# Attention scores on two row groups, exponentials by pairs of batches, and a new order on TensorE

## The reference

```python
q, k, v = per-head maps of plin(xm, w_q, b_q), plin(xm, w_k, b_k), plin(xm, w_v, b_v)
scores = jnp.einsum('bhqd,bhkd->bhqk', qt, kt) / math.sqrt(HD)
attn = jax.nn.softmax(scores, axis=-1)
out_h = expmap0(jnp.einsum('bhqk,bhkd->bhqd', attn, vt))
attn_out = plin(_from_heads(out_h), w_o, b_o)
```

## Time and profile before

| | us |
|---|---|
| median of 3 runs | 1287.87 (1287.47 to 1288.47) |
| profiled execution, its own time | 1287.52 |
| its span, first to last instruction | 1285.7 |
| TensorE busy | 1096.9 (85%) |
| VectorE busy | 1040.2 (81%) |
| ScalarE busy | 853.4 (66%) |
| GpSimd busy | 605.3 (47%) |

### The profile page before, as it was taken

The page is one execution under the profiler, slowest core; times in us unless marked ns, Lnnn a source line. Parts: engine busy times, 40 slices in busy tenths (PEclk is TensorE's granted clock), DMA queues, the critical chain, the costliest instruction groups (busy, mean ns, idle before and its releaser), DMA issues.

```text
span 1285.7 us, 20138 instructions
## 1 busy us (share of the span) xinstructions
PE 1096.9 (85%) x5760; PEld 783.9 (61%) x5782; DVE 1040.2 (81%) x2502; ACT 853.4 (66%) x2310; POOL 605.3 (47%) x1059
## 2 busy tenths in 40 slices
PE   8999967875895499999999999999988688888885
PEld 7888833332442287777777777777776345555554
DVE  6887758887787467888888888888987789989984
ACT  3545467877884246666666666666666788888873
POOL 2345236663575524334433444433421356667764
PEclk9999979997997799999999999999998889989998
DMA  7334221424976333334333433334225346666633
GB/s 246 105 112 103 97 81 45 176 111 144 375 232 187 98 99 82 99 99 98 86 88 91 99 88 89 87 99 99 60 61 127 67 97 164 164 164 165 164 99 115
DMA packets 116287, 156.32 MB, mean 122 GB/s; under 512 B 9296, under 2 KB 99536, under 8 KB 114640
## 3 DMA queue, kind: packets, MB, share of 16 engines
q1 hardware_dynamic: 115632, 155.03, 43.8%
q10 hardware_dynamic: 544, 0.00, 0.0%
HBM read 111.22 MB, written 27.00 MB: 108 GB/s over the span
## 4 chain that ended last, share of the span: by engine, by line
issue 24%; POOL 16%; PE 12%; DVE 9%; ACT 7%; POOLq 0%; DVEq 0%; ACTq 0%
POOL t_qk L1972 5%; POOL t_u L1902 4%; PE t_bk L1395 3%; POOL t_u L1907 3%; PE t_fB L1416 2%; PE t_bk L2034 1%; PE t_fA L2048 1%; ACT t_vbd L1460 1%; DVE t_qt L1628 1%; ACT t_vbd L1476 1%; ACT t_junk L1434 1%; PE t_bk L2022 1%; DVE t_bmax L1635 1%; PE t_fA L1378 1%; ACT t_y L1523 1%
## 5 line engine op out<-in xcount | busy, mean ns | idle before, releaser
L2034 PEld LDWEIGHTS t_bk<-t_vbd,t_pt 128*128 128x128 f32 x1024 | 133.4, 194 | 30.5 <-issue 19.3
L2034 PE MATMUL t_bk<-t_vbd,t_pt 128*128 128x66 f32 x1024 | 131.4, 273 | 18.5 <-ACT t_pt L2152 13.9
L2022 PE MATMUL t_bk<-t_qbd,t_kpar 128*128 128x256 f32 x512 | 135.9, 388 | 0.5 <-DMA t_qbd<-t_qt 0.5
L1395 PE MATMUL t_bk<-k_w12g,t_ut 128*128 128x512 f32 x256 | 126.5, 618 | 2.4 <-ACT t_ut L1516 1.2
L2022 PEld LDWEIGHTS t_bk<-t_qbd,t_kpar 128*128 128x128 f32 x512 | 92.8, 192 | 10.7 <-DMA t_qbd<-t_qt 0.9
L411 POOL TENSOR_SCALAR s_hleak<-s_hring,k_leak 128x128 f32<-128x128 f32 x128 | 47.6, 372 | 100.6 <-ACT s_hring L366 93.6
L2146 ACT ACTIVATE t_ysq<-t_y 128x768 f32<-128x768 f32 x64 | 53.8, 841 | 60.0 <-DVE t_y L2325 60.0
L2048 PE MATMUL t_fA<-k_wqkv,t_ut 128*128 128x512 f32 (+1 forms) x256 | 91.2, 500 | 1.2 <-ACT t_ut L2129 1.2
L1913 POOL TENSOR_SCALAR t_s_su<-t_s_ru 128x4 f32<-128x4 f32 x16 | 3.8, 236 | 180.8 <-ACT t_s_ru L2137 180.8
L2048 PE MATMUL t_fB<-k_wqkv,t_ut 128*128 128x512 f32 (+1 forms) x256 | 88.6, 489 | 0.0
L2152 ACT ACTIVATE t_pt<-t_bk 128x512 f32<-128x512 f32 x128 | 73.7, 587 | 21.7 <-PE t_bk L2022 20.2
(11 more groups left out here) (377 smaller groups left out, 3069.6 us busy)
## 6 DMA issues: line engine op xcount, KB each, us to landing
t_scb<-g_rows SPq DMA_DIRECT2D x64, 256.0 KB, 4.6
t_shb<-g_rows SPq DMA_DIRECT2D x64, 256.0 KB, 5.5
hidden_rows<-k_own SPq DMA_DIRECT2D x6, 1536.0 KB, 5.8
s_xrow<-in_x_dram SPq DMA_DIRECT2D x16, 512.0 KB, 3.6
k_hs<-s_hring SPq DMA_DIRECT2D x16, 512.0 KB, 3.1
b_xin<-in_x_dram SPq DMA_DIRECT2D x16, 512.0 KB, 4.4
x_rows<-b_xout SPq DMA_DIRECT2D x16, 512.0 KB, 5.1
t_xf<-x_rows SPq DMA_DIRECT2D x16, 512.0 KB, 4.7
```

The costliest lines, as they stand in the source:

```text
L1395: last = nc.tensor.matmul(z.fW[:, j, :], z.ut[:, c, j * P:(j + 1) * P], k["w12g"][:, c, :], start=False, stop=(c == C - 1))
L2022: last = nc.tensor.matmul(bk[e % 2][:, c * 4 * T:(c + 1) * 4 * T], kpar[:, c, e, :, :].rearrange("p a t -> p (a t)"), qbd[:, c, :, e * T:( ...
L2034: last = nc.tensor.matmul(bk[2 + e % 2][:, p * VW:(p + 2) * VW], pt[:, e % 2, p * T:(p + 2) * T], vbd[:, j, h, p:p + 2, :].rearrange("p c ...
```

## The change

A pair `n` of batches takes the place of a batch in `scores` and in the exponentials.

- Scores: for each batch and half `c`, instead of one product over 128 rows and 256 columns there are two, over rows 0 to 63 and 64 to 127, with 128 columns each. Rows 0 to 63 go with the pairs of heads 0 and 1 into bank 0, rows 64 to 127 with the pairs 2 and 3 into bank 1 (in the other columns `qbd` is zero in these rows). So both banks are filled by one pair of batches.
- Exponentials: one of 1024 columns over banks 0 and 1 for a pair. There are two tiles for them: `ptile`, of 1024 columns, and the tile `qt`, used again while it holds no queries. The next scores wait for the exponential before.
- Values: the same products, that read the new places.
- Order on TensorE: scores and values by pairs among the four products; the second stage's `turn_u` stands before the last two values in turn 16; the transposes of `qk` come after those of `u` and `o`, all four banks together, row tile by row tile for banks 0 and 1, each waiting for its own part of `qk`.
- Order on ScalarE: the four exponentials stand where those of batches 0, 2, 3 and 5 stood; `ut` is copied before `ot`.
- The numbers in the waits follow the new counts.

```diff
-                def scores(e):
-                    if e == 0:
+                def scores(n):
+                    if n == 0:
                         pe.wait_ge(s["qbd_loaded"], i * (4 * 16))
                         pe.wait_ge(s["kpar_ready"], i * (2 * C))
-                    if e >= 2:
-                        pe.wait_ge(s["exp_ready"], (i - 1) * GB + (e - 1))
-                    for c in range(C):
-                        last = nc.tensor.matmul(bk[e % 2][:, c * 4 * T:(c + 1) * 4 * T], kpar[:, c, e, :, :].rearrange("p a t -> p (a t)"),
-                                                qbd[:, c, :, e * T:(e + 1) * T], start=True, stop=True)
+                    else:
+                        pe.wait_ge(s["exp_ready"], (i - 1) * EPAIRS + n)
+                    for e in (2 * n, 2 * n + 1):
+                        for c in range(C):
+                            for r in range(2):
+                                rows, at = slice(r * T, (r + 1) * T), (e % 2 * C + c) * 2 * T
+                                last = nc.tensor.matmul(bk[r][:, at:at + 2 * T], kpar[rows, c, e, :, :].rearrange("p a t -> p (a t)"),
+                                                        qbd[rows, c, 2 * r:2 * r + 2, e * T:(e + 1) * T], start=True, stop=True)
                     last.then_inc(s["score_ready"], 1)
...
-                for e in range(GB + 1):
-                    if i == NG and e == 7:
-                        once(second.turn_u, 0)
-                    if mid and e < GB:
-                        scores(e)
-                    if mid and e >= 1:
-                        values(e - 1)
-                    if front and e < GT - 1:
-                        products(e + 1)
...
+                if mid:
+                    for n in range(2, EPAIRS):
+                        scores(n)
+                        values(2 * n - 2)
+                        values(2 * n - 1)
+                if i == NG:
+                    once(second.turn_u, 0)
+                if mid:
+                    values(GB - 2)
+                    values(GB - 1)
                 if head:
                     turn_x(i + 1)
...
                 if front:
-                    for b in range(C, 2 * C):
-                        turn_qk(b)
+                    if mid:
+                        pe.wait_ge(s["exp_ready"], i * EPAIRS)
+                    for half in range(2):
+                        for j in range(GT):
+                            if half == 0:
+                                pe.wait_ge(s["qk_ready"], i * GT + j + 1)
+                            for b in (2 * half, 2 * half + 1):
+                                last = nc.tensor.transpose(bk[b][:, j * P:(j + 1) * P], qk[:, j, b * P:(b + 1) * P], k["ident"][:, :])
+                                if j == GT - 1:
+                                    last.then_inc(s["qkt_ready"], 1)
...
-                def exponentials(e):
-                    act.wait_ge(s["score_ready"], (i - 1) * GB + (e + 1))
-                    if e >= 2:
-                        act.wait_ge(s["pv_ready"], (i - 1) * GB + (e - 1))
-                    nc.scalar.activation(pt[:, e % 2, :], bk[e % 2][:, :], ACT.Exp, scale=1.0 / math.sqrt(HD)).then_inc(s["exp_ready"], 1)
+                def exponentials(n):
+                    act.wait_ge(s["score_ready"], (i - 1) * EPAIRS + (n + 1))
+                    if n >= 2:
+                        act.wait_ge(s["pv_ready"], (i - 1) * GB + 2 * (n - 1))
+                    nc.scalar.activation(pt[n % 2], bank[:, 0:2, :].rearrange("p r n -> p (r n)"), ACT.Exp, scale=1.0 / math.sqrt(HD)).then_inc(s["exp_ready"], 1)
```

More of the change, by code:

```diff
@@ L49 @@
 NBLK = D // BLK
+EPAIRS = GB // 2
 QMAX = 127.0
@@ L1530, in turned_xd @@
         elif self.t:
-            act.wait_ge(self.t["score_ready"], NG * GB)
+            act.wait_ge(self.t["score_ready"], NG * EPAIRS)
         for c in range(C):
@@ L1703, in attention_mlp @@
         vbd = m.sb("vbd", [P, GT, 2, PAIRS, VW])
-        pt = m.sb("pt", [P, 2, 2 * D])
+        ptile = m.sb("pt", [P, 4 * D])
         rden = m.sb("rden", [P, 2, PAIRS // 2, 2])
@@ L1751, in attention_mlp @@
         flat_qt = qt[:, :, :].rearrange("p c r -> p (c r)")
+        pt = (ptile[:, :], flat_qt)
         flat_qbd = qbd[:, :, :, :].rearrange("p c q r -> p (c q r)")
@@ L2031, in values @@
                         pe.wait_ge(s["o_ready"], 2 * ((i - 1) * GB + e - 1))
-                    pe.wait_ge(s["exp_ready"], (i - 1) * GB + (e + 1))
+                    pe.wait_ge(s["exp_ready"], (i - 1) * EPAIRS + (e // 2 + 1))
                     for p in range(0, PAIRS, 2):
-                        last = nc.tensor.matmul(bk[2 + e % 2][:, p * VW:(p + 2) * VW], pt[:, e % 2, p * T:(p + 2) * T],
+                        at = (p % 4 // 2 * 4 + e % 2 * C + p // 4) * 2 * T
+                        last = nc.tensor.matmul(bk[2 + e % 2][:, p * VW:(p + 2) * VW], pt[e // 2 % 2][:, at:at + 2 * T],
                                                 vbd[:, j, h, p:p + 2, :].rearrange("p c w -> p (c w)"), start=True, stop=True)
@@ L2050, in products @@
                     last.then_inc(s["qkv_ready"], 1)
[L2052 to L2056, removed]
                 if front:
                     products(0)
-                for e in range(GB + 1):
-                    if i == NG and e == 7:
-                        once(second.turn_u, 0)
-                    if mid and e < GB:
-                        scores(e)
-                    if mid and e >= 1:
-                        values(e - 1)
-                    if front and e < GT - 1:
-                        products(e + 1)
-                if front:
-                    pe.wait_ge(s["qk_ready"], (i + 1) * GT)
-                    if mid:
-                        pe.wait_ge(s["exp_ready"], i * GB)
-                    for b in range(C):
-                        turn_qk(b)
+                if mid:
+                    scores(0)
+                if front:
+                    products(1)
+                if mid:
+                    values(0)
+                    values(1)
+                if front:
+                    products(2)
+                if mid:
+                    scores(1)
+                if front:
+                    products(3)
+                if mid:
+                    for n in range(2, EPAIRS):
[4 more added lines that the diff above has]
+                    once(second.turn_u, 0)
+                if mid:
+                    values(GB - 2)
+                    values(GB - 1)
                 if head:
@@ L2191, in turn @@
                 for e in range(GB):
-                    if mid:
-                        exponentials(e)
+                    if mid and e in (0, 2, 3, 5):
+                        exponentials((0, 2, 3, 5).index(e))
                     if front and e < GT:
@@ L2219, in turn @@
                         scaled_a()
+                if head:
+                    turned_u(i + 1)
+                if i == NG:
+                    once(second.turned_u, 0)
                 if mid:
@@ L2224, in turn @@
                                              fB[:, cc * GR:(cc + 1) * GR].rearrange("p (e c t) -> p e c t", c=C, t=T), ACT.Copy).then_inc(s["ot_ready"], 1)
-                if head:
-                    turned_u(i + 1)
-                if i == NG:
-                    once(second.turned_u, 0)
                 if front:
```

10 lines of the change are left out of this document (5 added, 5 removed).

## The result

| | median of runs | ratio to before, 95% interval |
|---|---|---|
| before | 1288.45 us (9 runs) | |
| after | 1297.42 us (9 runs) | 1.0069 [1.0042, 1.0097] |

A forecast was written before the change was run, and what follows sets the result against it. It took a ring through VectorE, TensorE, ScalarE and GpSimd, 34.02 us a turn, as the bound. First turn -2.0, middle turns -1.0, clock +2.3, last turn -3.0 gave -3.7 on a span of 1285.7: 1284 us, range 1277 to 1308.

The forecast's parts named there:

- Scores: TensorE's score products: a pair of batches falls from 1.72 to 0.87 us, plus about 0.1 for each of two row changes.
- Rival 2: Score products: row groups don't overlap, a pair costs 1.74 + 0.2 us, adding 1.5 a turn; 1307 us, chance 0.26.
- Exponentials: ScalarE: four of 1024 columns at 1.1 us replace eight of 512 at 0.587; 4.4 instead of 4.7 us, beside the ring.
- the ring: Attention turn from T, the first `t_y`: eighth output at 24.39, `kpar` 2.19 later, next `t_y` after 7.44; 34.02 to become 33.95.
- TensorE's tail: Transposes ending a middle turn: eighth output at T+24.13, `kpar` 2.38 later, 0.07 us gained a turn, -1.0 over 14 turns.
- First turn: Turn 0: `qk` is turned part by part, `kpar` starts at about 452.4 instead of 454.81; -2.0 us.
- The clock: TensorE's gap before the last half of `o`: a fall to 1.2 GHz in one of 14 turns, +2.3 us, bounds 0 and +31.
- rival 3: Middle turns: row groups overlap, but the clock falls in the gap in half of the turns, 15 us; 1297, chance 0.12.
- The last turn: Turn 16: the last output ends near 986 at full clock, 987.5 at low, against 989.93; -3.0 us, bounds -4 and +1.
- Rival 1: Attention loop: TensorE was the bound and all its saving shows, 14 x -3.5 = -49 us; 1236, chance 0.06.

The follow-up runs named there:

- e12_full_busy: e6_busy with the row groups undone: score products over 128 rows, half of them zeros; 1301.4 us, ratio 1.0105 to before.
- e2_gap: The changed kernel with idle transposes on TensorE in turns 1 to 15, before the last two value products and the last half of `o`; 1291.4 us.
- e6_busy: The changed kernel with the idle transposes of e2_gap in turns 1 to 15, and others in turn 16; 1284.3 us, ratio 0.9973 to before.
- e9_all_busy: The changed kernel with query transposes between the halves of `o`, idle transposes after them, before the last two value products and in turn 16; 1272.8 us.
- e7_before_busy: The kernel before with idle transposes in turn 16 alone, before the first and third value products; 1284.4 us, ratio 0.9968 to before.

## Why the prediction was wrong

**Scores: right.** 0.87 + 0.2 a pair was forecast, 1.09 measured; the same products with 128 rows take 1.79. The trace of after shows the overlap itself: the 16 records start in eight couples, 7 ns apart within a couple and 0.11 us from couple to couple, and the loads do the same; behind the first couple and behind the last it is 0.2 us, the price of 0.1 for each change. Rival 2's condition was not met, and the Trainium skill's sentence that products on different row groups run concurrently (TensorE: Matmul & The Clock Gate, part 3) holds here, loads included.

**Exponentials: right,** 1.00 to 1.02 us instead of 1.1. The forecast gave the pairs no cost on the ring; they would have had one (e12_full_busy, +0.85 on the eighth output), which the row groups cover.

**TensorE's tail: the size was right, the choice behind it was not seen.** 2.38 was measured, with some luck: the parts that the prediction lists add up to 2.34. The eighth output came at T+24.34, not 24.13, so a turn is 34.15 and not 33.95. With 14 turns that is +1.8 instead of -1.0. The cost of the query transposes and the gain of the early copy of `ut` stood in one sum, 2.38 against 2.19; taken apart they are +0.87 and -0.68 (the second by difference, no run has it alone).

**First turn: right.** -2.2 over turns 0 and 1, -2.0 forecast; its distance alone went from 27.04 to 24.59, and the next turn gave 0.2 back.

**The clock: the step that failed.** "I allow one in 14 turns: +2.3 in bounds of 0 and +31." The mechanism was named, and rival 3 with half of the turns at 1297 gave the time, but for a partly different reason. The clock fell in every middle turn, not in one of 14, and mostly earlier than supposed: at the last two value products, after the 1.03 us gap, not in the gap before `o`. In the profiled execution it was up again in time in turns 1 and 3 to 13, which are no longer than in e2_gap; turns 2 and 14 paid 1.7 and 2.3, together 4.0 where 2.3 was put. Turn 15, for which no clock was put at all, took 3.1 more to its `kpar` than before; only a part of that is the clock, since e6_busy, with a short low stretch, still has +2.3 there, and e9_all_busy, with none and another order, +1.0. With the clock held there e2_gap is 6.0 us faster in the medians; its profile is 3.5 us shorter in turns 2 to 14. In it and in e6_busy turn 15 still meets the low clock (16 query and key transposes take 3.24 in e6_busy). Why the clock falls in the changed kernel's middle turns, and in none of them before, stays open.

**The last turn: the other failed step.** "At full clock the last output ends near 986, at the low clock 987.5. I take -3.0." The low clock was allowed one short stretch. It held for 20.5 us, from the first value products on, and from `kpar` to the last output turn 16 took 29.73 instead of 27.66. At full clock (e6_busy) it is 23.70. But from T of turn 15 to the last output before takes 55.48 and e7_before_busy 52.93, which has no pairs; e6_busy takes 53.82, and 52.67 where turn 15 keeps its clock (e9_all_busy). What I had put down to the pairs was the low clock that the kernel before meets there, and the pairs gain 0.3 us at most.

**Rival 1: false.** With 2.5 us less of score products and the clock at 1.00, the turn of e6_busy is 0.13 us longer than before. TensorE's total work did not bound the loop; its clock reaches the ring by the last transposes. (Its figure of 1236 also takes the 49 us off the span instead of the time, which would give 1239.)

## What to carry to other kernels

Work taken off an engine that is nearly full but not on the ring bought nothing here, and the gaps that it left on TensorE cost: before such a change, look which products come after its new gaps and what they would take at 1.2 GHz, in the last turn of a pipelined loop above all, where half of the work has already gone. Cut the ring into terms at full clock and ask of each instruction that moves on which side of the last arrival it stands: eight transposes set behind the awaited half of `o` cost their whole length, 0.87 us, in every turn. Where the clock is the loss, idle transposes in the gaps can give it back: 13 us here, and 15 in the better order.

## What the runs showed of the hardware

- Two row groups load and stream side by side: 16 f32 records of 64 rows and 128 columns took 1.09 us up to the next product, changes of row tiling included, and started two by two, 7 ns apart; 16 of 128 rows took 1.79, one each 0.11 us.
- The clock fell from 2.4 to 1.2 GHz in ordinary turns of after with no gap longer than 1.15 us since it had last risen (from 549.92 to 580.64 us), and one of 1.03 just ahead. Before had gaps of 1.02 and 0.80 in a turn and stayed at 1.00 over 600 to 934. What in the changed kernel tips it was not taken apart.
- Idle f32 transposes in the gaps held the clock: with them it was 1.00 over 600 to 934, where after had 0.94, and the middle turns of e6_busy are longer than the ordinary ones of after by 0.03 us at most (e6_busy and e9_all_busy below). The Trainium skill (TensorE: Matmul & The Clock Gate, part 4, PE-mode transpose), whose figures there are for bf16, says that the full clock does not engage for transposes, which don't count as busy in the same way; these traces differ, and eight transposes took 1.04 us at 1.00 and 1.91 at 0.50:

```profile
600.00:934.00 334.00, 319.64 (x2274) 255.26 (x2273) 287.61 (x636) 216.24 (x572) 137.38 (x266) 1.00 0.37 90
```

```profile
600.00:934.00 334.00, 326.01 (x2301) 257.67 (x2297) 296.87 (x656) 221.34 (x586) 136.81 (x269) 1.00 0.38 92
```

- The four operations of `moved` on VectorE take 3.43 us where they took 3.28, with the same shapes. Their neighbours on the other engines have moved; the cause was not tried.
